# Attention inside the kernel: a small TensorE tile for each batch and head in place of block-diagonal operands

## The chip, the cores and the metric

One core of one Trainium2 chip runs the whole program. The metric is the device time of one execution in microseconds; several executions are made and the median is given. All data is f32.

## What is computed

A language-model tower of depth one: 4 x 512 tokens, 256 channels, 4 heads of 64. A row of a table is gathered for each token, then comes an attention-like layer with a recurrent state, and then a layer in which each token goes through one of 8 experts. The change lies in the attention layer. Cut to what matters:

```python
xx = shift(x) - x                      # xr, xw, xk, xv, xa, xg = x + xx * x_...
r, k, v = xr @ Wr, xk @ Wk, xv @ Wv
w = -softplus(-(w0 + tanh(xw @ w1) @ w2)) - 0.5
v = v + (v - v) * sigmoid(v0 + xv @ v1 @ v2)
a = sigmoid(a0 + xa @ a1 @ a2);  g = sigmoid(xg @ g1) @ g2
kk = normalised_per_head(k * k_k);  k = k * (1 + (a - 1) * k_a)
def step(S, ...):                      # S: 64 x 64 for each batch and head, over 512 steps
    sa = S @ (-kk)
    S = S * exp(-exp(w)) + outer(sa, kk * a) + outer(v, k)
    y = S @ r
y = (y - mean) / sqrt(var + 0.00064) * ln_w + ln_b      # per head
y = (y + sum(r * k * r_k) * v) * g @ Wo
```

## The kernel before, in words

The 512 steps are computed in chunks of 32 tokens (L). A chunk of all four batches is 128 rows; two chunks (CH) make a slab, and there are 8 slabs (SLABS). Within a chunk the recurrence is a triangular system of 32 x 32 for each batch and head; it is inverted by doubling, in four levels, and the state S is carried from chunk to chunk.

Each engine has its own program. All of them are written by the same function `pipeline`, which walks through one list of step names, `ORDER`, once for each turn. The letter ahead of a name says which slab the step works on in that turn (AHEAD): F, the layer norm and the transposes of the slab two ahead; P, all projections, gates, decay and the matrices of the slab one ahead; Q, the inversion and the state of this slab; O, norm and output of the slab behind. Engines wait for each other by semaphores only. So the order in which TensorE takes P and Q steps is the order of the list. Turns 1 to 4 are two rounds of a loop that holds two turns, the others are written out.

The steps that matter here, with their lines on TensorE: P.k, P.r, P.v (L877), the low-rank pairs (L883 down, L888 up), sums over heads (L894, with matrices of ones), P.tok (L997, six times four transposes that bring v, k and b to tokens), P.M (L977, products within a chunk for each batch and head), Q.X (L1009) and Q.T (L1018), the two matmul groups of one level of the inversion, Q.W (L1032, L1036), Q.A (L1048) and Q.S (L1059 to L1070), the right side, the solution, the new state and the output y, O.mean, O.var (L894), O.out (L1086). In a level, X is masked by VectorE (L680), T is added (L685) and transposed (L689), and ScalarE (L431) and GpSimd (L310) copy the blocks into `u_bd`. The operands of Q are block-diagonal: a unit holds four blocks of 32 x 32 on the diagonal of a 128 x 128 weight, two batches by two heads, and the slab has 8 units (UN). The same holds for the state, `state_bd`, with blocks of 64. In the last slab, where nothing else is left to do, `idle` puts matmuls without use (L903) between the steps of Q.

```python
                    for u in range(UN):
                        last = mm(ps[:, 4, u * L:(u + 1) * L], n_bd[par][:, u, :], t_c[:, u, :], start=True, stop=True)
```

## Time and profile before

| | us |
|---|---|
| three runs | 737.79, 733.80, 750.32 (median 737.79) |
| the profiled execution, first to last instruction | 741.3 |
| busy: TensorE matmul / weight load | 642.5 / 529.5 |
| busy: VectorE / ScalarE / GpSimd | 401.1 / 290.9 / 133.1 |
| mean granted clock of TensorE, share of 2.4 GHz | 0.886 |

A record is one instruction in the trace. An f32 matmul of the program appears as two MATMUL records with a LDWEIGHTS record each, a transpose as one. In a group, `128*128` is rows by columns of the stationary operand, `128x32` the streamed one.
### The profile page before, as it was taken

To read this page: it belongs to the slowest core of one execution; us is meant where nothing else is said; L and a number is where in the kernel's file an instruction comes from. 1 tells how busy PE (TensorE), PEld (TensorE's weight loads), DVE (VectorE), ACT (ScalarE), POOL (GpSimd) and SP (SyncE) were. 2 spreads that over 40 slices of the span, in tenths; PEclk is the share of its full clock that TensorE was granted. 3 is DMA by queue.
4 is the path that set the end of the run, shared out by engine and by line. 5 is a ranking of instruction groups with operands and counts; after the bars stand their busy time and mean duration, and the time that the engine had idled before them with its cause. 6 is when DMAs were issued, how large, how long until landed. Compare 5 with 4: busy or idle time off the path is not lost.

```text
span 741.3 us, 11776 instructions
## 1 busy us (share of the span) xinstructions
PE 642.5 (87%) x4339; PEld 529.5 (71%) x4340; DVE 401.1 (54%) x851; ACT 290.9 (39%) x556; POOL 133.1 (18%) x122
## 2 busy tenths in 40 slices
PE   0879899999998999999999999899948389999930
PEld 0658898888887889889888979899925145666620
DVE  6674576577676577677666765532163531222212
ACT  1554644354553464563545454511214003333300
POOL 6603102200400220130130040011000350000034
PEclk9979899599998989998979997999958558999985
DMA  7500000000000000000000000000009521212126
GB/s 216 187 1 1 1 2 1 0 2 1 1 1 3 1 1 1 1 1 2 1 1 1 1 1 1 2 1 1 1 2 399 203 92 44 63 64 64 56 60 188
DMA packets 20702, 30.95 MB, mean 42 GB/s; under 512 B 3832, under 2 KB 16432, under 8 KB 20528
## 3 DMA queue, kind: packets, MB, share of 16 engines
q1 hardware_dynamic: 18320, 23.99, 9.3%
q0 software_dynamic: 2336, 6.30, 2.8%
q8 instruction: 34, 0.56, 0.3%
q14 instruction: 12, 0.10, 0.0%
HBM read 20.06 MB, written 10.22 MB: 41 GB/s over the span
## 4 chain that ended last, share of the span: by engine, by line
PE 79%; DVE 8%; ACT 5%; issue 3%; POOL 2%; DMA 1%; SPq 1%; POOLq 0%; DVEq 0%
PE ps L1018 8%; PE ps L1009 7%; PE ps L877 6%; PE ps L1153 6%; PE ps L1170 5%; PE ps L888 5%; PE ps L883 5%; PE ps L1070 4%; PE ps L903 3%; PE ps L894 3%; PE ps L1048 3%; PE ps L997 3%; PE ps L1059 2%; PE ps L1133 2%; PE ps L1086 2%
## 5 line engine op out<-in xcount | busy, mean ns | idle before, releaser
L310 POOL TENSOR_TENSOR arena<-arena 64x512 f32<-64x512 f32 x40 | 48.9, 1224 | 401.0 <-DVE arena L689 201.4
L1018 PEld LDWEIGHTS ps<-arena 128*128 128x128 f32 x512 | 63.7, 200 | 11.4 <-DVE arena L680 5.6
L431 ACT COPY arena<-arena 32x256 f32<-32x256 f32 x80 | 32.3, 404 | 93.0 <-DVE arena L689 81.4
L1009 PEld LDWEIGHTS ps<-arena 128*128 128x128 f32 x512 | 64.5, 199 | 4.8 <-issue 2.6
L1018 PE MATMUL ps<-arena 128*128 128x32 f32 x512 | 65.4, 283 | 2.5 <-DVE arena L680 2.5
L1009 PE MATMUL ps<-arena 128*128 128x32 f32 x512 | 63.0, 278 | 0.0
L877 PE MATMUL ps<-arena 128*128 128x256 f32 x192 | 50.4, 410 | 6.5 <-issue 3.1
L877 PEld LDWEIGHTS ps<-arena 128*128 128x128 f32 x192 | 37.9, 204 | 13.0 <-issue 4.0
L448 ACT COPY arena<-arena 64x512 f32<-64x512 f32 x32 | 19.8, 618 | 68.2 <-PE ps L1070 68.0
L685 DVE TENSOR_TENSOR arena<-ps,arena 128x256 f32<-128x256 f32 x32 | 13.6, 424 | 59.1 <-PE ps L1018 59.0
L1153 PE MATMUL ps<-arena 128*128 x92 | 45.2, 614 | 0.1
L894 PE MATMUL ps<-arena 128*128 128x256 f32 x128 | 39.8, 439 | 5.6 <-ACT arena L452 3.3
L1170 PE MATMUL ps<-arena 128*128 x184 | 43.8, 379 | 0.8 <-ACT arena L496 0.8
L549 DVE SCALAR_TENSOR_TENSOR arena<-arena 128x256 f32<-128x256 f32 x96 | 41.0, 477 | 5.3 <-remote 2.7
L888 PE MATMUL ps<-arena 64*128 64x256 f32 (+2 forms) x128 | 41.7, 453 | 0.0
L839 DVE TENSOR_TENSOR arena<-ps,arena 128x512 f32<-128x512 f32 x23 | 15.9, 691 | 46.6 <-PE ps L1153 46.6
L1070 PE MATMUL ps<-arena 128*128 128x32 f32 x256 | 37.3, 269 | 0.0
L1170 PEld LDWEIGHTS ps<-arena 128*128 128x128 f32 x184 | 33.2, 190 | 5.3 <-issue 1.5
L883 PE MATMUL ps<-arena 128*64 128x256 f32 (+2 forms) x128 | 36.2, 408 | 0.0
L330 POOL DMA_INDIRECT arena<-sorted_o,arena x16 | 15.7, 979 | 112.8 <-DMA sorted_o<-arena 108.3
L680 DVE TENSOR_TENSOR arena<-ps,arena 128x256 f32<-128x256 f32 x32 | 13.4, 418 | 38.6 <-PE ps L1009 38.3
L894 PEld LDWEIGHTS ps<-arena 128*128 128x128 f32 x128 | 24.9, 211 | 12.8 <-issue 3.6
(189 smaller groups left out, 1305.9 us busy)
## 6 DMA issues: line engine op xcount, KB each, us to landing
arena<-W SPq DMA_DIRECT2D x16, 512.0 KB, 9.5
sorted_x<-arena SPq DMA_DIRECT2D x1, 2944.0 KB
arena<-sorted_x SPq DMA_DIRECT2D x23, 128.0 KB, 2.0
sorted_o<-arena SPq DMA_DIRECT2D x23, 128.0 KB, 1.7
arena<-b SPq DMA_DIRECT2D x1, 2048.0 KB, 20.3
out<-arena SPq DMA_DIRECT2D x16, 128.0 KB
arena<-W SPq DMA_DIRECT2D x4, 256.0 KB
arena<-consts SPq DMA_DIRECT2D x7, 64.0 KB
```

Of the source, the lines that this page charges most:

```text
L310: nc.gpsimd.tensor_tensor(u_bd[low, :, 64:128].rearrange("p u (q t) -> p u q t", q=2), (u_c if lvl else u_0[par])[low].unsqueeze(2).broadc ...
L431: last = nc.scalar.copy(u_bd[rows, :, L * q:L * q + L], (u_c if lvl else u_0[par])[rows])
L549: last = V.scalar_tensor_tensor(out=mix[j % 3][:, p, :], in0=xx[:, p].rearrange("p b t -> p (b t)"), scalar=vec[name][:, p:p + 1], in1=xT[ ...
L877: last = mm(ps[:, bank, m * NT:(m + 1) * NT], w[:, kt, m * 128:(m + 1) * 128], src[:, kt, :], start=kt == 0, stop=kt == 1)
L883: last = mm(ps[0:rows, bank, 0:NT], w[:, kt, :], src[:, kt, :], start=kt == 0, stop=kt == 1)
L888: last = mm(ps[:, bank, m * NT:(m + 1) * NT], w[0:rows, m * 128:(m + 1) * 128], src[0:rows, :], start=True, stop=True)
L894: last = mm(ps[:, bank, p * NT:(p + 1) * NT], w, src[:, p, :], start=True, stop=True)
L1009: last = mm(ps[:, 4, u * L:(u + 1) * L], n_bd[par][:, u, :], t_c[:, u, :], start=True, stop=True)
L1018: last = mm(ps[:, 5, u * L:(u + 1) * L], u_bd[:, u, :], x_c[:, u, :], start=True, stop=True)
L1070: last = mm(ps[:, 7, x + e * L:x + (e + 1) * L], state_bd[:, 2 * k + e, :], ar[par][:, k // 2, c * B + 2 * (k % 2) + e, L:2 * L], start=Fa ...
L1153: last = mm(ps[:, 2 + b, :], x_sT[b][:, p, :], W1_sb[:, bass.ds(e * (2 * HID) + p * HID, HID)], start=p == 0, stop=p == 1)
L1170: last = mm(ps[:, 6 + b, 0:C], hT[b][:, m, :], W2_sb[:, bass.ds(e * (HC * C) + m * C, C)], start=m == 0, stop=m == HC - 1)
```

## The change

Every batch and head gets a tile of TensorE of its own. The four batches of a chunk stand in partitions 0-31, 32-63, 64-95 and 96-127 (`quarter(b)`), and a product within a chunk is a matmul of 32 x 32 or 64 x 32 weights that reads and writes only those. Nothing is spread on a diagonal any more, and the copies that did so on ScalarE, GpSimd and VectorE are gone. r, k, kk, a and the decays lie by channel of one head (64) in two halves for the parity of the batch (`headed`), values, gates, y and z lie by token (`by_token`). The decay sums are matmuls against a triangle (P.cum) instead of a scan on VectorE. v is brought to mean zero per head (`vc`) ahead of the state, so y needs no mean; its variance is a square on ScalarE and a reduction on VectorE. In a level, T and its transpose U both come from matmuls, so VectorE doesn't transpose. low w and low a share one step (P.lwa). Part of S and y is computed ahead of the solution (in Q.A and Q.W). `idle` is gone. `set_up` puts one more wait, on a semaphore that is long past, ahead of a group of small tiles. The list ORDER is new.

The diff, cut to what the prediction speaks of:

```diff
-UN = 2 * CH * 2
+UN = CH * H
+GR = 2 * H
+SL = CH * L
...
-ORDER = """Q.start P.k O.mean P.r Q.X0 P.v Q.T0 P.lv P.vd O.var Q.X1 P.lw P.vg Q.T1 P.vgate O.z1 P.la P.w Q.X2 O.z2 P.lg P.a Q.T2
-P.vbd F.stats P.g O.out0 P.decay F.rstd Q.X3 P.norm F.xn O.out1 P.inv Q.T3 O.add Q.W0 F.xT Q.A0 P.tok0 P.tok1 P.key Q.S0 P.ar Q.W1
-P.rt P.kbd P.bonus Q.A1 P.tok2 P.tok3 P.bbd Q.S1 P.vcmp P.tok4 P.tok5 P.M F.xx P.ve Q.yT P.masks""".split()
+ORDER = """P.k Q.X0 O.sq Q.T0 P.r O.red Q.X1 P.v O.yn Q.T1 P.lv P.lwa Q.X2 P.kk P.vg O.zT Q.T2 P.wup P.lg Q.X3 F.stats P.a Q.T3
+P.g P.cum O.out P.decay F.rstd Q.W0 P.norm O.add Q.A0 F.xn P.key Q.S0 F.xT P.ar P.rt Q.W1 P.kP P.tokk Q.A1 P.bP P.tokb Q.S1 P.vc P.q F.xx
+P.M P.masks""".split()
...
-                    V.tensor_tensor(t_c, ps[:, 5, 0:UN * L].rearrange("p (u t) -> p u t", u=UN), t_c, ALU.add).then_inc(s["t_ok"], 1)
-                    dve.wait_ge(s["t_ok"], 5 * i + lvl + 2)
-                    dve.wait_ge(s["ubd_ok"], 5 * i + lvl + 1)
-                    dve.wait_ge(s["ubd2_ok"], 5 * i + lvl + 1)
-                    V.transpose(u_c.rearrange("p u t -> p (u t)"), t_c.rearrange("p u t -> p (u t)")).then_inc(s["u_ok"], 1)
...
+            def mul(out_, lhsT, rhs, start, stop):
+                return nc.tensor.matmul(out_, lhsT, rhs, start=start, stop=stop, skip_group_check=True)
...
+            def headed(w, src, bank):
+
+                for h in range(H):
                     for kt in range(2):
-                        last = mm(ps[:, bank, m * NT:(m + 1) * NT], w[:, kt, m * 128:(m + 1) * 128], src[:, kt, :],
-                                  start=kt == 0, stop=kt == 1)
+                        for e in range(2):
+                            to = ps[half(e), bank, :].rearrange("p (h b c t) -> p h b c t", b=2, h=H, c=CH)[:, h]
+                            last = mul(to, w[:, kt, half(h)], of_parity(src[:, kt, :], e), kt == 0, kt == 1)
                 return last
...
+            def to_tokens(src, bank):
+
+                for c in range(CH):
+                    for h in range(H):
+                        for b in range(B):
+                            g, e, u = h * 2 + b // 2, half(b % 2), c * H + h
+                            last = mul(ps[quarter(b), bank, u * HS:(u + 1) * HS], src[e, g, c, :], ident[e, e], True, True)
                 return last
-
-            def idle(i, count):
-
-
-                if isinstance(i, int) and i == SLABS - 1:
-                    pe.wait_ge(s["tok_ok"], 6 * SLABS)
-                    for _ in range(count):
-                        mm(ps[:, 0, 0:NT], cst["ones_bd"], w_sb["k"][:, 0, :], start=True, stop=True)
 
             def emit(step, i, par):
                 n = i + 1
...
-                    for src, bank in ((b_bd, 2), (k_bd, 3)):
-                        for p in range(2):
-                            for u in range(BLK):
-                                q, col = 64 * (u % 2), ((p * BLK + u) // 2) * 2 * L
-                                last = mm(ps[q:q + 64, bank, col:col + 2 * L], src[:, p, u, :], ar[par][:, p, u, :],
-                                          start=True, stop=True)
-                    last.then_inc(s["m_ps"], 1)
...
+                    for src, bank in ((bP, 2), (kP, 3)):
+                        for c in range(CH):
+                            for h in range(H):
+                                for b in range(B):
+                                    g, e, u = h * 2 + b // 2, half(b % 2), c * H + h
+                                    last = mul(ps[quarter(b), bank, u * 2 * L:(u + 1) * 2 * L], src[e, g, c, :], ar[par][e, g, c, :],
+                                              True, True)
+                        last.then_inc(s["m_ps"], 1)
...
                     for u in range(UN):
-                        last = mm(ps[:, 4, u * L:(u + 1) * L], n_bd[par][:, u, :], t_c[:, u, :], start=True, stop=True)
+                        for b in range(B):
+                            q = quarter(b)
+                            last = mul(ps[q, 4, u * L:(u + 1) * L], n_b[par][q, u, 0:L], u_m[q, u, :], True, True)
                     last.then_inc(s["x_ps"], 1)
-                    idle(i, 3)
...
                     for u in range(UN):
-                        last = mm(ps[:, 5, u * L:(u + 1) * L], u_bd[:, u, :], x_c[:, u, :], start=True, stop=True)
+                        for b in range(B):
+                            q = quarter(b)
+                            last = mul(ps[q, 6, u * L:(u + 1) * L], y_t[q, u, :], t_m[q, u, :], True, True)
+                            if lvl < 3:
+                                last = mul(ps[q, 6, (UN + u) * L:(UN + u + 1) * L], t_m[q, u, :], y_t[q, u, :], True, True)
                     last.then_inc(s["t_ps"], 1)
-                    idle(i, 5)
...
-                    for k in range(4):
-                        mm(ps[:, 4, k * HS:(k + 1) * HS], mak_bd[par][:, unit(k // 2, c, 2 * (k % 2)), :],
-                           v_cmp[par][:, unit(k // 2, c, 2 * (k % 2)), :], start=k == 0, stop=False, skip_group_check=True)
-                    for k in range(4):
-                        for e in range(2):
-                            last = mm(ps[64 * e:64 * e + 64, 4, k * HS:(k + 1) * HS], a_bd[par][:, k // 2, c * B + 2 * (k % 2) + e, :],
-                                      state[:, 2 * k + e, :], start=False, stop=k == 3, skip_group_check=True)
-                    last.then_inc(s["w_ps_c"], 1)
-                    idle(i, 3)
...
+                    for h in range(H):
+                        for b in range(B):
+                            q, u, at_h = quarter(b), c * H + h, half(h)
+                            mul(ps[q, 4, at_h], m_k[par][q, u, 0:L], vc[par][q, c, at_h], h == 0, False)
+                            mul(ps[q, 5, c * C + h * HS:c * C + (h + 1) * HS], m_k[par][q, u, L:2 * L], vc[par][q, c, at_h],
+                               c == 0 and h == 0, False)
+                    set_up()
+                    if c:
+                        pe.wait_ge(s["s_ok0"], n)
+                    for h in range(H):
+                        for b in range(B):
+                            g, e = h * 2 + b // 2, half(b % 2)
+                            last = mul(ps[quarter(b), 4, half(h)], ar[par][e, g, c, 0:L], state[e, b // 2, half(h)], False, True)
+                    last.then_inc(s["w_ps"], 1)
+                    for h in range(H):
+                        for b in range(B):
+                            g, e = h * 2 + b // 2, half(b % 2)
+                            mul(ps[quarter(b), 5, c * C + h * HS:c * C + (h + 1) * HS], ar[par][e, g, c, L:2 * L], state[e, b // 2, half(h)],
+                               False, False)
...
+                    for h in range(H):
+                        for b in range(B):
+                            q = quarter(b)
+                            last = mul(ps[q, 4, C + h * HS:C + (h + 1) * HS], t_m[q, c * H + h, :], w_s[q, half(h)], True, True)
                     last.then_inc(s["sa_ps"], 1)
-                    idle(i, 5)
...
+                        for b in range(B):
+                            q = quarter(b)
+                            mul(ps[half(b % 2), 6 + b // 2, half(h)], k_tok[par][q, c * H + h, :], vc[par][q, c, half(h)], h == 0, False)
...
-                    for k in range(4):
-                        u, x = unit(k // 2, c, 2 * (k % 2)), k * 128
-                        mm(ps[:, 6, x:x + 128], k_tok[par][:, u, :], v_e[par][:, u, :], start=True, stop=False)
-                        last = mm(ps[:, 6, x:x + 128], b_tok[par][:, u, :], sa_e[:, k, :], start=False, stop=True)
+                    set_up()
+                    pe.wait_ge(s[f"sa_ok{c}"], n)
+                    for h in range(H):
+                        for b in range(B):
+                            q = quarter(b)
+                            last = mul(ps[half(b % 2), 6 + b // 2, half(h)], b_tok[par][q, c * H + h, :], sa[q, half(h)], False, True)
...
+                    for h in range(H):
+                        for b in range(B):
+                            q = quarter(b)
+                            last = mul(ps[q, 5, c * C + h * HS:c * C + (h + 1) * HS], n_b[par][q, c * H + h, L:2 * L], sa[q, half(h)],
+                                      False, True)
```

The first place is the start of a turn on TensorE: P.k, then the first levels of the inversion. Before (a row is a line, an operation, output partitions by streamed columns, and a count in matmuls of the program):

```order
L877 MATMUL ps<-arena 128x256 x4
L1006 REGISTER_ALU
L1007 ISA
L1009 MATMUL ps<-arena 128x32 x8
L929 REGISTER_ALU
L877 MATMUL ps<-arena 128x256 x4
L1014 ISA
L1018 MATMUL ps<-arena 128x32 x8
```

And now, where all matmuls but transposes stand in the helper's line L801:

```order
L801 MATMUL ps<-arena 64x128 x16
L801 MATMUL ps<-arena 32x32 x96
L860 REGISTER_ALU
L801 MATMUL ps<-arena 64x128 x16
L801 MATMUL ps<-arena 32x32 x32
L865 REGISTER_ALU
L801 MATMUL ps<-arena 128x256 x4
L801 MATMUL ps<-arena 32x32 x64
```

X0 and T0 (8 matmuls each before) are 32 and 64, and stand together (the 96), where P.r or P.v stood between two steps of the inversion.

The second place is the end of a turn on TensorE, the second chunk's solution, its state and y, and the matrices P.M. Before:

```order
L1070 MATMUL ps<-arena 128x32 x2
L997 MATMUL ps<-arena 128x128 x8
L977 MATMUL ps<-arena 64x64 x32
L201 UNCONDITIONAL_BRANCH
L201 ISA
```

Now, from the sum with r_k (P.rt) on:

```order
L801 MATMUL ps<-arena 32x1 x32
L801 MATMUL ps<-arena 32x64 x112
L801 MATMUL ps<-arena 64x64 x16
L801 MATMUL ps<-arena 32x64 x32
L801 MATMUL ps<-arena 64x64 x16
L801 MATMUL ps<-arena 32x64 x80
```

The 112 are W1 (64), the token copies of k (32) and A1 (16); the last 80 are the y part of S1 (16) and P.M (64).

The third place is VectorE between the state of the second chunk and the end of the turn. Before, and then now:

```order
L701 TENSOR_TENSOR arena<-ps,arena 128x512
L705 TENSOR_TENSOR arena<-arena 128x512
L676 TENSOR_TENSOR arena<-arena 128x512
L591 TENSOR_TENSOR arena<-arena 128x16x31
L592 TENSOR_TENSOR arena<-arena 128x16
L549 SCALAR_TENSOR_TENSOR arena<-arena 128x256 x4
L658 TENSOR_TENSOR arena<-ps,arena 128x256
L662 TENSOR_TENSOR arena<-ps,arena 128x1024
```

```order
L635 TENSOR_TENSOR arena<-ps,arena 128x512
L639 TENSOR_TENSOR arena<-arena 128x512
L601 TENSOR_REDUCE arena<-arena 128x8
L603 SCALAR_TENSOR_TENSOR arena<-arena 128x512
L546 TENSOR_TENSOR arena<-arena 128x16x31
L547 TENSOR_TENSOR arena<-arena 128x16
L513 SCALAR_TENSOR_TENSOR arena<-arena 128x256 x4
L609 TENSOR_TENSOR arena<-ps,arena 128x512
L611 TENSOR_TENSOR arena<-arena 128x256
L614 TENSOR_TENSOR arena<-ps,arena 128x512
L616 TENSOR_TENSOR arena<-arena 128x256
L618 STREAM_TRANSPOSE arena<-arena 128x256
```

The reduction and the subtraction of v's mean (L601, L603) stand between the state and the mixes; the masks are narrower than before (no 1024 columns).

## Rows read from the trace of the kernel before

**Rows 1.** Stretches: start:end, length, busy (count) by engine, clock, DMA.

```profile
50.50:476.80 426.30, 415.48 (x3263) 365.13 (x3264) 279.28 (x527) 209.69 (x409) 71.33 (x56) 0.92 0.00 1
478.80:534.70 55.90, 55.90 (x403) 52.35 (x401) 17.67 (x33) 9.01 (x20) 5.79 (x5) 1.00 0.00 1
...
556.00:741.00 185.00, 135.02 (x547) 86.89 (x547) 57.06 (x177) 46.21 (x82) 31.27 (x32) 0.80 0.35 123
```

**Rows 2.** Line L977 in the source view: durations in ns, first and last start.

```profile
L977 PE MATMUL ps<-arena x512: 222/222/271, 50.5 to 476.8; 128*64 128x64 f32 x171
```

**Rows 3.** TensorE's waits from 50.5 to 476.8: total us, times, longest.

```profile
PE ps L1048 <- ACT arena L435: 4.1, 10, 0.7
PE ps L877 <- issue: 3.1, 1, 3.1
PE ps L1018 <- DVE arena L680: 2.5, 3, 1.9
PE ps L877 <- DVE arena L664: 0.4, 1, 0.4
```

**Rows 4.** Timeline of TensorE in the last slab: start, length, line, shapes, count.

```profile
482.86 1.87 PE L1009 MATMUL ps<-arena 128*128 128x32 f32 x16
484.57 1.54 PE L903 MATMUL ps<-arena 128*128 128x256 f32 x6
...
504.81 1.03 PE L1086 MATMUL ps<-arena 128*128 128x256 f32 x4
505.67 1.87 PE L1009 MATMUL ps<-arena 128*128 128x32 f32 x16
```

**Rows 5.** Timeline of TensorE around L977; the last row from its first 20 ns.

```profile
50.22 0.38 PE L997 MATMUL ps<-arena 128*128 128x128 f32 x2
50.53 2.08 PE L977 MATMUL ps<-arena 128*64 128x64 f32 x64
52.55 0.48 PE L877 MATMUL ps<-arena 128*128 128x256 f32 x1
...
50.53 0.28 PE L977 MATMUL ps<-arena 128*64 128x64 f32 x2
```

**Rows 6.** Stretches around a fall of the clock (columns as in rows 1).

```profile
125.10:128.50 3.40, 3.40 (x24) 2.70 (x22) 1.14 (x5) 1.25 (x4) 0.00 (x0) 1.00 0.02 5
128.50:145.60 17.10, 17.10 (x56) 13.41 (x55) 8.90 (x15) 5.78 (x13) 5.95 (x4) 0.50 0.00 0
```

**Rows 7.** Timeline of TensorE over the same stretches.

```profile
125.86 1.97 PE L1018 MATMUL ps<-arena 128*128 128x32 f32 x16
127.77 1.27 PE L883 MATMUL ps<-arena 128*64 128x256 f32 x4
...
138.38 3.62 PE L1018 MATMUL ps<-arena 128*128 128x32 f32 x16
141.81 2.05 PE L888 MATMUL ps<-arena 128*128 128x256 f32 x4
```

**Rows 8.** Groups by line: shapes, count, busy us, mean ns, idle before.

```profile
L1009 PE MATMUL ps<-arena 128*128 128x32 f32 x512 | 63.0, 278 | 0.0
...
L549 DVE SCALAR_TENSOR_TENSOR arena<-arena 128x256 f32<-128x256 f32 x96 | 41.0, 477 | 5.3 <-remote 2.7 <-issue 2.4
...
L680 DVE TENSOR_TENSOR arena<-ps,arena 128x256 f32<-128x256 f32 x32 | 13.4, 418 | 38.6 <-PE ps L1009 38.3
...
L701 DVE TENSOR_TENSOR arena<-ps,arena 128x512 f32<-128x512 f32 x16 | 11.1, 691 | 13.0 <-PE ps L1060 12.8
...
L467 ACT ACTIVATE arena<-arena 128x512 f32<-128x512 f32 x8 | 5.0, 630 | 0.3
```

**Rows 9.** Timeline of the end of the attention stage.

```profile
535.77 0.58 PE L1070 MATMUL ps<-arena 128*128 128x32 f32 x4
...
541.74 4.66 DVE L718 BATCH_NORM_STATS2 arena<-arena 128x6 f32<-128x256 f32 x14
...
553.09 0.69 DVE L734 TENSOR_TENSOR arena<-ps,arena 128x512 f32<-128x512 f32 x1 [3.87 <-PE ps L1086]
```

855 lines of the change are left out of this document (401 added, 454 removed).

## Prediction

> **What bounds the kernel now.** I read the stretches first [rows 1]. The attention stage in its steady state runs from 50.5 to 476.8 us, and TensorE is busy for 415.48 of those 426.30 us. So TensorE sets the pace there. Everything else stands below it: VectorE 279, ScalarE 210, GpSimd 71. The source view of L977 gives the period [rows 2]. Its 512 records are 8 bursts of 64, one per slab, and the first and the last burst start 426.3 us apart, so a turn takes 426.3 / 7 = 60.9 us. The waits confirm the first reading [rows 3]: in all seven turns TensorE waits 10.1 us for anything.
>
> What fills a turn is the number of TensorE records times their spacing. (An f32 matmul of the program leaves two records, a transpose one.) Starts in the timeline give the spacings [rows 4]. Sixteen records of L1009 (32 streamed columns over 128 stationary ones) start at 482.86 and the next line starts at 484.57: 0.107 us each. Four records of L1086 (256 streamed columns) take 0.86, so 0.215 each. The 64 records of L977 (64 stationary columns, two outputs side by side in partitions 0-63 and 64-127) run from 50.53 to 52.55: 0.0316 each [rows 5].
>
> Per turn that is 284 records at 0.11 (X and T 128, W, A and the state 64, the y part 64, transposes 28) = 31.2; 80 at 0.215 = 17.2; 96 at 0.0316 = 3.0. Together 51.4 of 60.9. The other 9.5: waits 10.1/7 = 1.4, about 20 changes of tile shape, and above all stretches at the lower clock. From 128.5 on TensorE works at half its clock for 17 us [rows 6], and 16 records of L1018 then take 3.43 (138.38 to 141.81) where they took 1.91 (125.86 to 127.77) [rows 7]. The mean clock of the seven turns is 0.92 [rows 1]; a sixth of the time at half clock loses about 34 us, 4.9 per turn.
>
> **The change, part by part.** No block-diagonal operands means small weights and many more matmuls. Records per turn afterwards:
>
> - Wide ones: v 8, low v 4, the joined low w and a 8 (two tiles side by side, so 4 in time), v, w and g gates 12, low g 4, out 8, the norm as one 512-column matmul 2 (4 in time): 44 x 0.215 = 9.5.
> - k, r and a: 80 records with 128 streamed columns on two 64-column tiles. One such stream alone is half of 0.215; side by side, as L977 does it, 0.055: 4.4.
> - Transposes of xn and z: 8 x 0.11 = 0.9.
> - Small ones: decay sums 64, r_k sum 64, token copies of k and b 128, M 128, X 256, T 448, W 256, A 128, S 128 = **1600**.
>
> Removed are the 128 wide X and T records, the 64 of the y part, 24 transposes, and three of four head sums. So 14.8 us stand fixed, and the price of the 1600 decides.
>
> **Price of a small record.** No row of before has it. From above: the mean of L977, 0.0316, which is two tiles wide. From below: L977 has two tiles, and each tile gets a record every 0.063. Two of its records start at once after a wait: a pair takes 0.28, one alone 0.27 [rows 2, 5]. So the starts of two tiles can lie 0.01 apart, and what spaces L977 is the tile and not the queue. Four tiles then give 0.0158 for the 832 records of 64 columns, and half, 0.0079, for the 768 of 32 columns or fewer: 19.2 us, a mean of 0.0120. I take 0.014, near the lower end, because the row shows the tile as its limit, with a little for the queue: 22.4 us. Both ends stay for the range: 19.2 and 50.6 us per turn.
>
> The Trainium skill, "TensorEngine Tiling (Array Packing)", section Instruction Overhead, speaks against this: each matmul has an overhead of about 60 cycles, and one streamed column lasts as long as 60. By that, taken as a gap between any two matmuls at 2.4 GHz (25 ns), the 1600 would cost 40 us per turn and the kernel would come to about 770 us; the trace has no 32-column stream on a small tile and cannot say.
>
> **Changes of shape.** Entering L977 costs 0.09 over the plain spacing: the last two transposes start at 50.22, at 0.11 each the next record would start at 50.44, and L977 starts at 50.53 [rows 5]. The changed order has about 36 such changes in a turn, 3.6 us.
>
> **Waits that the new order exposes.** VectorE operations of 512 columns take 0.69, of 256 columns 0.42 to 0.48, a ScalarE Exp of 512 columns 0.63, and the tail of a matmul, start to end, is 0.28 [rows 8]; I allow 0.1 per handing over. (1) T0 stands right behind X0 on TensorE, with nothing between: tail, one mask, handing over = 0.9. Queued behind it are P.r and all of the turn. (2) The sum r_k (rt) waits for norm, max, Ln, Exp, and four VectorE operations of 0.69: 0.27 + 0.69 + 1.26 + 2.76 + 0.7 = 5.7; beside it TensorE has 128 small records (1.8) and four transposes (0.4): 3.4 exposed. The second half of W and the token copies stand behind it. (3) The first X waits for the masks. From S1 on VectorE does the state (1.4), vc (1.3), xx (0.85), four mixes (1.9), masks with one transpose (2.65), in all 8.9 with handing over; TensorE has the rest of S, M and P.k, 0.45 + 1.8 + 1.8: 4.9 exposed. Sum 9.2. The other seven X and T steps are covered by P steps of 0.9 or more. If small records cost more, (2) and (3) shrink.
>
> VectorE itself: 28 operations at 0.69, 24 at 0.45 and small ones make 31 us a turn against 279.28/7 = 39.9, ScalarE falls from 30 to about 20, GpSimd stays near 10. None of them is a bound.
>
> A turn: 14.8 + 22.4 + 3.6 + 9.2 = 50.0; for the clock I keep 2 instead of 4.9, since there is less wide work to lose: **52.0**. Seven turns: 7 x 8.9 = 62 us less.
>
> **The ends.** The last slab's inversion has no other work beside it. Before, it fills with dummy matmuls (L903) and takes 478.8 to about 535.9, 57 us [rows 1, 9]. After: a level is X 0.9 + tail and mask 0.9, T 1.8 + 1.26, four levels 18; the two chunks 5.1 each; 29 us. Without dummies the clock will fall there; I take 24 less, not 28. Then the output: from y at 536.3 to 553.8 [rows 9], with two wide sums, ten passes and 14 statistics; after it has a square, a sum, three passes and the same statistics, 5 less. The first slab and everything behind 556 stay: the routing and expert code is the same, its 185 us too.
>
> Sum on the profiled execution: 741.3 - 62 - 24 - 5 = 650. Its span is 3.5 above the median of the three runs (737.79), so **647** on their scale.
>
> **The rivals.**
>
> *A, the queue sets the spacing.* If records cannot follow each other faster than at some spacing, whatever the tile, each nanosecond of it costs 1600 x 7 = 11.2 us. The gain is gone at 0.014 + 91/11.2 = 0.022; at 0.0316, the row's own value, the time is 844. Halfway, at 0.027, it is 647 + 13 x 11.2 = 793. For it: the highest rate anywhere in the trace is that of L977. Against: the close starts. Chance 0.27, of it slower 0.17, same 0.05, faster 0.05.
>
> *B, the clock.* From 125.1 to 128.5 TensorE was busy for all of 3.40 us and the clock fell after it [rows 6]. What ran was mostly short streams, L1018 with 32 columns [rows 7]. Small tiles stream over a quarter of the rows. If half of the time is at 0.5, the wide part gains 7.5 and the tile-bound small part about 8 per turn: 52 + 15.5 - 2 = 65.5, so 7 x 4.6 = 32 more, 29 less, on the scale of the median 741. For: the level falls without any idle time. Against: L1036 and L977 ran at full clock. The Trainium skill ("TensorE: Matmul & The Clock Gate", section HAM oscillation) blames idle gaps; rows 6 show a fall without one. Chance 0.12: slower 0.05, same 0.04, faster 0.03.
>
> *C, the chain through VectorE is longer than I count*. With every operation handed over at 0.25 instead of 0.1, some 45 of them, a turn grows by 7 us: 696. For: VectorE is strictly in order and the exposed waits all go through it. Against: its 31 us fill only 60% of a turn. Chance 0.10: faster 0.09, same 0.01.
>
> *D, my forecast*, 605 to 700, chance 0.51, all faster.
>
> **How the numbers follow.** A measurement of this kernel tells about 2% from no change, so faster is below 723 and slower above 752. Faster 0.51 + 0.09 + 0.05 + 0.03 = 0.68, same 0.10, slower 0.22. The lower end 605 is 0.0120 with half of the exposed waits (5 less each turn). The upper end reaches into A to 0.0254: 775, which leaves out about 0.14 above and 0.05 below.
>
> **What would show it.** In the changed profile the bursts of the T steps (128 records) should take 1.8 us, X 0.9, M 1.8. If T takes 3 or more at full clock, A holds. The period between two M bursts should be 52 with VectorE around 31 busy. Granted clock in the seven turns below 0.8 with T bursts near 1.8 would be B. VectorE waits for TensorE should be small at L622 and L630, and TensorE's waits should name the last of the key operations (L585) and the masks (L618). A busy ScalarE above 25 a turn, or a last slab over 40 us, would contradict my account of the ends. I am wrong altogether if tiles with the same output bank do not run side by side: then a small record costs more than L977's.

## The result, and the profile after

The changed kernel takes **705.9 us** (median of 4 runs, 700.7 to 710.3) against 737.9: a ratio of 0.957, 95% interval 0.950 to 0.963. That is faster by 4%, inside the whole range given (605 to 775, above the 700 up to which I counted it as my own case) and in its direction, but a third of the 91 us that I had forecast. Executions more than 1.5% above the fastest of their kernel are left out of the ratios, not of the medians. Two further sets of runs of it (after_again, control_3) gave ratios of 0.960 (0.948 to 0.971) and 0.938 (0.930 to 0.946), medians 705.1 and 698.3.

The profiled execution spans 708.5 us. From its page, first the busy times, then the queue that brings instructions, and two shares of the chain of work that ended last:

```profile
PE 524.5 (74%) x14419; PEld 404.3 (57%) x14420; DVE 296.9 (42%) x662; ACT 187.6 (26%) x372; POOL 133.2 (19%) x117
...
q8 instruction: 113, 1.85, 1.1%
...
PE 67%; issue 13%; DVE 12%; ACT 2%; POOL 2%; DMA 2%; SPq 2%; POOLq 0%; DVEq 0%
```

TensorE has 14,419 matmul records where it had 4,339, and is busy for less of the span. 13% of the chain is "issue", time in which an engine waited for nothing that the profile shows. The page of the kernel before has 3% there and 34 packets on q8.

The stretches, with the columns of [rows 1]. The first X burst of the first slab starts at 56.77 and that of the last slab at 464.58, so the first row is seven turns; then the last slab's inversion and chunks, then its output:

```profile
56.77:464.58 407.81, 325.53 (x12091) 264.83 (x12091) 191.13 (x367) 118.53 (x245) 73.88 (x55) 0.87 0.02 4
464.58:504.70 40.12, 26.84 (x1225) 22.80 (x1228) 8.48 (x15) 2.59 (x7) 0.00 (x0) 0.66 0.01 4
504.70:519.40 14.70, 5.12 (x28) 3.30 (x17) 8.90 (x21) 2.98 (x5) 0.00 (x0) 0.54 0.01 2
```

A turn is 407.8 / 7 = 58.3 us, where it was 60.9 and I had 52.0. TensorE is busy for 80% of it, where it was for 97%. Its waits over the seven turns, against [rows 3]:

```profile
PE ps L801 <- issue: 67.8, 71, 3.8
PE ps L801 <- DVE arena L618: 7.5, 7, 1.9
PE ps L801 <- ACT arena L432: 3.1, 5, 1.3
PE ps L801 <- DVE arena L513: 2.9, 5, 0.7
PE ps L801 <- DVE arena L622: 0.6, 1, 0.6
```

TensorE lost 82 us to waits instead of 10, and five sixths of it has no releaser. Where it sits is seen in the timeline of one turn's end (start, length, line, shapes, count, and in brackets the idle time ahead of the row):

```profile
275.04 1.38 PE L801 MATMUL ps<-arena 64*32 64x1 f32 x77
277.79 2.24 PE L801 MATMUL ps<-arena 32*32 32x64 f32 x127 [1.37 <-issue]
281.72 3.00 PE L801 MATMUL ps<-arena 64*32 64x64 f32 x127 [1.70 <-issue]
285.45 0.84 PE L801 MATMUL ps<-arena 64*32 64x64 f32 x13 [0.73 <-issue]
```

The idle times cut through bursts that wait for nothing: the last three rows begin in the middle of Q.W1, of P.tokk and of P.tokb. Between two of them stand 127 or 128 matmul records. Each record has its weight load, so that is 256 TensorE instructions. A packet on q8 is 16 KB, which would be 256 instructions of 64 bytes: the 113 packets x 256 are 28,900, about TensorE's own count of 28,839 (14,419 + 14,420), and the 34 of the kernel before are 8,704, against 8,679. In the trace such packets start at 275.61, 279.00 and 282.95, and TensorE goes on at 277.79, 281.72 and 285.45, some 2.5 us behind each. This gave the theory that the experiments were to test.

**Theory F**: TensorE runs dry. Its instructions come in blocks of 256 that cannot follow each other faster than every 3.5 us, and a block of small matmuls is worked off in 1.1 to 1.9. **Theory R**, the rival: the gaps belong to the array, its tiles or its clock, and the number of instructions does not matter.

### The profile page after: what moved, and what is told of

It reads as the page before. It is cut to its first block, busy times and chain, and to the rows that moved or that the text cites. A ratio compares the mean times of both kernels' runs of the same rounds, so it can differ in the third digit from the quotient of the medians.

```text
span 708.5 us, 31478 instructions
## 1 busy us (share of the span) xinstructions
PE 524.5 (74%) x14419; PEld 404.3 (57%) x14420; DVE 296.9 (42%) x662; ACT 187.6 (26%) x372; POOL 133.2 (19%) x117
## 3 DMA queue, kind: packets, MB, share of 16 engines
q8 instruction: 113, 1.85, 1.1%
## 4 chain that ended last, share of the span: by engine, by line
PE 67%; issue 13%; DVE 12%; ACT 2%; POOL 2%; DMA 2%; SPq 2%; POOLq 0%; DVEq 0%
PE ps L801 46%; PE ps L1119 6%; PE ps L1136 6%; PE ps L1099 2%; POOL arena L336 2%; PE ps L1127 1%; DVE arena L513 1%; PE ps L1073 1%; PE ps L1065 1%; SPq L229 1%; PE ps L1108 1%; PE ps L1048 1%; DVE arena L546 1%; PE ps L1080 1%; DMA arena<-g 1%
## 5 line engine op out<-in xcount | busy, mean ns | idle before, releaser
L801 PE MATMUL ps<-arena 32*32 32x32 f32 (+6 forms) x13808 | 376.9, 231 | 106.4 <-issue 83.2
L801 PEld LDWEIGHTS ps<-arena 32*32 32x32 f32 (+4 forms) x13808 | 307.0, 125 | 174.9 <-issue 147.0
L630 DVE TENSOR_TENSOR arena<-ps,arena 128x512 f32<-128x512 f32 (+1 forms) x32 | 19.9, 623 | 63.8 <-PE ps L801 63.6
L301 POOL TENSOR_TENSOR arena<-arena 128x512 f32<-128x512 f32 x8 | 9.5, 1186 | 179.5 <-ACT arena L364 179.5
L635 DVE TENSOR_TENSOR arena<-ps,arena 128x512 f32<-128x512 f32 x16 | 11.0, 687 | 71.4 <-PE ps L801 71.4
L1136 PEld LDWEIGHTS ps<-arena 128*128 128x128 f32 x184 | 33.2, 190 | 5.0 <-issue 1.5
L330 POOL DMA_INDIRECT sorted_x<-arena x16 | 15.6, 975 | 106.0 <-DVE arena L740 101.4
L766 DVE TENSOR_TENSOR arena<-ps,arena 128x512 f32<-128x512 f32 x23 | 15.9, 692 | 46.5 <-PE ps L1119 46.5
L622 DVE TENSOR_TENSOR arena<-ps,arena 128x256 f32<-128x256 f32 x32 | 13.6, 425 | 51.6 <-PE ps L801 51.6
L316 POOL TENSOR_TENSOR arena<-arena 128x512 f32<-128x512 f32 x8 | 17.5, 2192 | 84.8 <-ACT arena L420 84.8
L464 ACT COPY arena<-ps 128x256 f32<-128x256 f32 x23 | 8.6, 374 | 60.7 <-PE ps L1108 60.6
L1119 PEld LDWEIGHTS ps<-arena 128*128 128x128 f32 x92 | 16.1, 196 | 12.1 <-issue 12.1
L356 ACT COPY arena<-ps 128x512 f32<-128x512 f32 x8 | 4.7, 587 | 63.7 <-PE ps L801 53.7
L429 ACT COPY arena<-ps 128x256 f32<-128x256 f32 x16 | 6.0, 373 | 52.7 <-PE ps L801 52.7
L359 ACT COPY arena<-ps 128x512 f32<-128x512 f32 x8 | 4.7, 586 | 57.2 <-PE ps L801 57.2
L472 ACT COPY arena<-ps 128x512 f32<-128x512 f32 x23 | 13.5, 587 | 20.6 <-PE ps L1127 20.6
```

The source lines that it names most:

```text
L316: P.tensor_tensor(per_unit(rtv), per_unit(v2nd), rt.unsqueeze(2).broadcast_to([128, UN, HS]), ALU.mult).then_inc(s["rtv_ok"], 1)
L330: pool.indirect_dma_start(out=sorted_x[:, :], out_offset=bass.IndirectOffsetOnAxis(ap=place[:, t:t + 1], axis=0), in_=xn2[:, t, :], in_off ...
L472: nc.scalar.copy(hT[b], ps[:, 4 + b, :].rearrange("p (a t) -> p a t", a=HC)).then_inc(s["hT_ok"], 1)
L622: V.tensor_tensor(y_t, ps[:, 4, 0:UN * L].rearrange("p (u t) -> p u t", u=UN), cst["low"][:, L * lvl:L * lvl + L].unsqueeze(1).broadcast_t ...
L630: V.tensor_tensor(both, ps[:, 6, 0:wide * UN * L], both, ALU.add).then_inc(s[f"t_ok{lvl}"], 1)
L766: V.tensor_tensor(h_pre[b], ps[:, 2 + b, :], b1_sb[:, bass.ds(e * HID, HID)], ALU.add).then_inc(s["pre_ok"], 1)
```

## The experiments

For the comparisons I split each turn by the starts of the records: the spacing of each shape at full clock, what the half clock adds to it, changes of shape, gaps behind which stands a semaphore, and gaps over 0.3 us inside a burst without one. The turns here run from the second to the eighth norm matmul, six in all, us per turn. The wide records are the same in all of these kernels, so a difference of 1 us in that column is what the split gets wrong, and no finer reading rests on it:

| kernel | turn | wide | small | changes | clock | semaphore | gaps without | packets |
|---|---|---|---|---|---|---|---|---|
| changed (after_again) | 57.7 | 15.1 | 20.5 | 5.0 | 3.5 | 5.2 | 8.4 | 14.0 |
| half_count | 49.3 | 14.1 | 18.5 | 4.4 | 1.1 | 5.3 | 5.9 | 11.0 |
| double_columns | 57.6 | 14.1 | 23.8 | 4.4 | 1.7 | 6.3 | 7.2 | 14.0 |
| vector_transpose | 51.0 | 13.9 | 18.1 | 4.5 | 2.0 | 6.1 | 6.3 | 12.5 |
| gate_later | 58.9 | 14.9 | 20.3 | 4.9 | 4.2 | 7.2 | 7.4 | 14.0 |
| one_block_more | 61.2 | 14.1 | 21.6 | 5.0 | 4.7 | 6.0 | 9.8 | 15.0 |

### Fewer instructions, same columns; same instructions, more columns

```diff
 # half_count (X; T alike)
-for u in range(UN):
+for u in range(0, UN, 2):
-    mul(ps[q, 4, u * L:(u + 1) * L], n_b[par][q, u, 0:L], u_m[q, u, :], True, True)
+    mul(ps[q, 4, u * L:(u + 2) * L], n_b[par][q, u, 0:L], u_m[q, u:u + 2, :], True, True)
 # double_columns: u from 0 to 7 as before, each u writing the pair of places u - u % 2 and the next
```

> Edit: the changed kernel, but each X and T matmul streams 64 columns (two units) instead of 32, and there are half as many of them; the products are then not the reference's (each pair of units is multiplied by the first one's operand). Streamed columns are the same; 352 of about 1600 small TensorE records a turn are gone, with their weight loads 704 instructions, 2.75 blocks of 256. Theory F (TensorE runs dry because each 256 instructions need a fetched 16 KB block, and a block cannot come faster than every 3.5 us or so): the gaps of over 0.4 us on TensorE that no semaphore explains, 60.6 us in the seven turns of the changed kernel, fall below 30; instruction packets fall from 113 to about 93; time 655 to 672. Theory R (the gaps have to do with the array, its tiles or the clock, and the number of instructions does not matter): only the shorter bursts count, 704 records at 9.9 ns become 352 at 14.5 ns, 1.9 us less a turn, 13 in all, so about 693, with the gaps left at 50 to 60 us.

> Edit: the changed kernel, same number of X and T matmuls, but each streams 64 columns instead of 32 (it recomputes its neighbour's place as well, so the products are not the reference's). Instruction count unchanged, streamed columns of these 704 records a turn doubled: 9.9 ns to about 14.5 ns each, 3.2 us more array time a turn. Theory F: where a block's arrival sets the pace the longer work fits into the gap, so the gaps of TensorE without a semaphore fall from 60.6 to 40 to 50 us in the seven turns and the time grows by only 5 to 15 us: 711 to 721. Theory R: the whole of it is added, 3.2 x 8 = 26, 732, with the gaps as before.

Measured: half_count 626.9 us, ratio 0.851 (0.841 to 0.861). double_columns 694.9, ratio 0.942 (0.933 to 0.952). The page's line on the instruction queue, and the six turns, of half_count and then of double_columns:

```profile
q8 instruction: 91, 1.49, 1.0%
...
74.20:370.00 295.80, 244.24 (x8301) 196.43 (x8293) 165.66 (x324) 103.72 (x216) 62.35 (x47) 0.97 0.02 4
```

```profile
q8 instruction: 113, 1.85, 1.1%
...
84.40:429.80 345.40, 283.64 (x10407) 232.13 (x10405) 166.78 (x324) 103.52 (x215) 64.01 (x47) 0.95 0.02 4
```

Taking 352 records a turn away and leaving their columns takes 8.4 us from a turn, of which the small records are 2.0, the gaps 2.5 and the clock 2.4. The packets fell by 22, as 704 instructions less in each of eight slabs say. Doubling the columns of 704 records a turn adds 3.3 us of array time and nothing to the turn. R said 693 and 732 for the two, and both are far off. F's numbers missed too. It gave 655 to 672 and 711 to 721, so half_count gained more than it allows and double_columns did not lose the 5 to 15 us that it allows; and half_count's gaps, which it put below 30 us in seven turns, are 5.9 a turn, 41. What I had left out is in the table: in both the clock stands higher, 0.97 and 0.95 against 0.89, worth 2.4 and 1.8 us a turn. double_columns lies 3 to 11 us below the changed kernel in the other sets of runs, with no control of its own, so I read no gain from it, only that the added work cost nothing.

### A whole block more

First I tried it with 256 satisfied semaphore waits a turn, in both kernels (a satisfied wait is one on a semaphore that has long reached its value).

```diff
 def emit(step, i, par):          # TensorE; eight wide steps
+    if step in ['P.v', 'P.lv', 'P.lwa', 'P.wup', 'P.lg', 'P.g', 'O.out', 'P.norm']:
+        for _ in range(32):
+            pe.wait_ge(s["zeroed"], 1)
```

> Edit: the changed kernel with 32 further waits on a semaphore that is long satisfied ahead of each of 8 wide steps of TensorE (values, low ranks, gates, output, norm), 256 instructions a turn with no array work: one block more a turn. The result stays the reference's. Theory F: one instruction packet more a turn, 113 to about 121, and a turn grows by 1 to 3.6 us, 8 to 28 in all: 714 to 734. Theory R: a turn grows by the waits' own issue time alone, which the same waits in the kernel before give (their cost there is the control).

> Edit: the kernel before with the same 256 satisfied waits a turn, 32 ahead of each of 8 wide steps of TensorE. The result stays the reference's. It has about 1000 instructions a turn, 4 blocks in 60.9 us, so by theory F the fifth block is hidden and only the waits' own issue time shows: 256 at 0.01 us or less, under 3 us a turn: 738 to 755. Theory R says the same of this kernel; the difference to the changed kernel with the waits is what tells them apart: F gives the changed kernel the larger increase, R gives both the same.

Measured: waits_after 794.7 us, ratio 1.074 (1.063 to 1.086); waits_before 740.5, ratio 1.005 (1.001 to 1.008). The direction is F's, but 89 us are three times what it allows, so the experiment did not price a block. The traces show two reasons. The 32 waits ahead of a step became 16 instructions: TensorE's sequencer, the part that issues its instructions, has 1,024 more records than without them (1,787 against 763, and 1,784 against 760), and q8 has four packets more (117 and 38), not the eight that I had counted on. So only half a block a turn was added. And such an instruction is itself not cheap: in a row they start 0.106 us apart in both kernels, which is 128 x 0.106 = 13.6 us a turn. A turn of waits_after is 14.6 us longer (72.3 against 57.7), so the changed kernel pays for nearly all of it; the kernel before pays 0.3 a turn. So it was done again with work that costs the sequencer no more than what is there:

```diff
 # one_block_more, P.rt
-for c in range(CH):
+for c in (0, 1, 0, 1, 0, 1):
```

> Edit: the changed kernel, but the sum r_k (P.rt) is done three times over into the same place, which leaves the result as it is: 128 more records a turn with one streamed column, at 8.4 ns each 1.08 us of TensorE, and 256 more instructions, exactly one block, in the part of the turn where small bursts follow each other. Theory F: a block costs its arrival and not its work, 3.5 to 4 us a turn, 28 to 32 in all, 733 to 738. Theory R: 1.1 a turn, 8.6 in all, 714.

> Edit: none, the changed kernel, as the control of the two others on this chip: 700 to 710.

Measured: one_block_more 731.6, ratio 0.980 (0.973 to 0.988); control_3 698.3, ratio 0.938 (0.930 to 0.946). The ratios differ by 0.042 of the kernel before's 743 us: **31 us for eight blocks, 3.9 a block** (2.9 to 4.9 by the two intervals; the medians differ by 33), with 1.1 of array time in each. F had 28 to 32, R 8.6. The q8 line has 121 packets, eight more, and a turn is 61.2 us, 3.5 longer than in after_again and 4.1 longer than in control_3 (57.1).

### The rate by itself

```diff
 # rates, ahead of TensorE's first step: the same 512 matmuls (1024 records), 32 columns on 32x32
+for k in range(512): matmul(*one(k))                             # L805
+with pe.Fori(0, 16): for k in range(32): matmul(*one(k))         # L808, half a block
+with pe.Fori(0, 8): for k in range(64): matmul(*one(k))          # L811, one block
+with pe.Fori(0, 2): for k in range(256): matmul(*one(k))         # L814, four blocks
```

> Edit: the changed kernel with a measuring section ahead of TensorE's work: 512 f32 matmuls of 32x32 by 32 columns over the four row tiles in a straight line (1024 records, 2048 instructions, 8 blocks), the same 512 as a loop of 16 turns of 32 (half a block), of 8 turns of 64 (one block) and of 2 turns of 256 (4 blocks), then 128 matmuls of 128x128 by 128 columns. The result stays the reference's. Theory F: the straight line runs at 3.5 us a block, 27 ns a record, in steps of 128 records with a gap behind each, and the wide ones run without gaps; whether the short loops run from what is already there (9 to 10 ns a record but for the jump) or fetch each turn is open and is what this looks for. Theory R: the straight line runs at 9.9 ns a record without gaps.

The timeline of TensorE in that section:

```profile
42.35 1.93 PE L805 MATMUL ps<-arena 32*32 32x32 f32 x128 [2.08 <-issue]
45.81 1.93 PE L805 MATMUL ps<-arena 32*32 32x32 f32 x128 [1.53 <-issue]
49.27 1.93 PE L805 MATMUL ps<-arena 32*32 32x32 f32 x128 [1.53 <-issue]
52.73 0.69 PE L805 MATMUL ps<-arena 32*32 32x32 f32 x34 [1.53 <-issue]
53.19 14.80 PE L808 MATMUL ps<-arena 32*32 32x32 f32 x1024
68.08 11.18 PE L811 MATMUL ps<-arena 32*32 32x32 f32 x1024
79.33 1.49 PE L814 MATMUL ps<-arena 32*32 32x32 f32 x155
82.80 1.27 PE L814 MATMUL ps<-arena 32*32 32x32 f32 x128 [1.98 <-issue]
86.27 1.93 PE L814 MATMUL ps<-arena 32*32 32x32 f32 x128 [2.19 <-issue]
90.28 7.49 PE L814 MATMUL ps<-arena 32*32 32x32 f32 x613 [2.09 <-issue]
```

This settles it. In a straight line every 128 records stand 3.46 us apart (45.81, 49.27, 52.73), or 4.0. That line ran at half clock, where the records alone take 1.7 us (13.4 ns each); the loop of four blocks begins at full clock, where they take 1.1, and the step is again 3.47 (82.80, 86.27). The same matmuls as a loop of one block take 11.18 us for all 1024, at full clock, with a single packet at the loop's start (69.16) and 0.3 us for each jump back. The four-block loop has gaps on its first turn; its second, 512 records, is within the last row and runs through from 91.85 to 97.58 at 11 ns each, in part at half clock. So the gaps are the arrival of new instructions, and what was fetched can be run again without them.

> Edit: the changed kernel with another measuring section ahead of TensorE's work, behind the loading of the weights: in straight lines 512 records each with 32, 64 and 128 streamed columns on 32x32 tiles; then loops of 3 turns whose bodies are 6, 7.5 and 9 blocks of 256 instructions. The result stays the reference's. Theory F: with 32 and 64 columns (9 and 15 ns a record, 1.2 and 1.9 us a block) both straight lines take the same 3.5 us a block; with 128 columns (28 ns or more, 3.6 us a block) the gaps go. The 4-block loop of the run before had no gaps on its second turn; a body too large for what TensorE keeps has gaps on every turn, the others on the first alone. The main loop of the kernel before has about 8 blocks and fetches on every turn, so I expect the limit between 6 and 9 blocks. Theory R: the spacing follows the streamed columns from the start, 9, 15 and 28 ns, without gaps.

The straight lines of 64 and of 128 columns in rates_2 (here both L808), then the loop of six blocks from the last block of its first turn on. The row of 384 ends with 86 records of that loop's start, and the row of 1774 with records of the next loop's:

```profile
41.23 1.99 PE L808 MATMUL ps<-arena 32*32 32x64 f32 x128 [0.74 <-issue]
44.97 1.99 PE L808 MATMUL ps<-arena 32*32 32x64 f32 x128 [1.75 <-issue]
48.71 0.70 PE L808 MATMUL ps<-arena 32*32 32x64 f32 x35 [1.75 <-issue]
...
57.20 9.54 PE L808 MATMUL ps<-arena 32*32 32x128 f32 x384 [0.32 <-issue]
...
87.78 16.99 PE L808 MATMUL ps<-arena 32*32 32x32 f32 x1774
106.78 0.41 PE L808 MATMUL ps<-arena 32*32 32x32 f32 x27 [2.00 <-issue]
```

With 64 columns a block still takes 3.74 us (41.23, 44.97, 48.71), with 128 columns the records alone take 3.5 us a block (27 ns each) and the gap behind a block shrinks to 0.3. The second and third turns of the six-block loop (768 records each, to 102.5) run without a gap but for the jump. The loops of 7.5 and of 9 blocks had an idle time of 1.5 us or more behind every 128 records on all three turns. So of a loop TensorE keeps at least 6 blocks and fewer than 7.5. The attention loop of the changed kernel has 27 or 28 blocks (two turns) and that of the kernel before about 8, so both fetch everything each time; the kernel before needs a block only every 15 us and never notices.

### The order

```diff
-... P.a Q.T3 P.g P.cum O.out ... P.tokk Q.A1 ...
+... P.a Q.T3 P.cum O.out ... P.tokk P.g Q.A1 ...
```

P.g then waits for tokk_ok, the next P.lv for g_ok and F.xT for lg_ok.

> Edit: the changed kernel, same instructions, in another order: P.g (4 wide records, 0.75 us, few instructions for their time) stands behind P.tokk, between bursts of small records, instead of ahead of P.cum among wide ones. The result stays the reference's. Theory F: the 0.75 us and the change of shape come to lie in the gaps of the tail, 3 to 8 us less in all: 698 to 703 if the control gives 706. Theory R: no change within 2 us.

Measured: 715.1, ratio 0.968 (0.948 to 0.989), control 0.960 (0.948 to 0.971): the intervals overlap, so neither the gain of 3 to 8 us nor a loss is shown. In the profile the gaps did fall, by 1.0 us a turn, as F says. But waits on semaphores rose by 2.0. Of gate_later over its six turns:

```profile
PE ps L801 <- DVE arena L513: 7.4, 5, 2.3
...
PE ps L801 <- ACT arena L423: 4.7, 6, 0.8
```

The first, for the mixes of VectorE, was 2.8 in after_again. The second is new. L423 is ScalarE's copy of the key tokens, and P.g stands right behind the burst that feeds it. I had counted neither. As a test of F it is inconclusive.

### The last slab

```diff
 # before_no_fill: the dummies of L903 left out
 # after_fill, ahead of each Q.X and Q.T of the last slab
+    idle(i, 2)     # ones_bd x w_sb["k"], 256 columns, into bank 0
```

> Edit: the kernel before without the dummy matmuls (L903) of the last slab; the result stays the reference's. It prices the last slab's part of the change. If the dummies only keep the clock up, the last slab's X, T, W and A work (about 170 wide records, 20 us) then runs at half clock where it is not waiting, and the last slab (478.8 to 535.9) becomes 0 to 8 us longer. If they are in the way of the chain, it becomes up to 10 us shorter. In all 728 to 748.

> Edit: the changed kernel with two dummy matmuls (128x128 by 256 columns, 0.43 us each at full clock, 0.86 at half) ahead of each X and each T of the last slab, 16 in all; the result stays the reference's. In the changed kernel the last slab's inversion, 464.6 to 488.2 of its profile, runs wholly at half clock. By my prediction's term (4 us lost there for the clock) this gives 2 to 4 us back if the dummies fit into the waits of 0.8 to 1 us: 701 to 704. If theory F carries the last slab too (gaps of blocks 13 us of its 53), the clock does not matter and nothing changes: 704 to 708; if the dummies are in the way of the chain, 3 to 6 us more.

Measured: 750.0 us (733.1 to 755.4) and 693.6 (681.2 to 700.0); no ratio for either. So I read them by their stretches. First before_no_fill from its last L977 burst to its last product, then after_fill and control_3 from X0 to their last product:

```profile
470.80:536.20 65.40, 57.74 (x311) 54.83 (x307) 19.30 (x35) 10.51 (x23) 5.79 (x5) 0.58 0.00 1
```

```profile
449.65:486.93 37.28, 27.75 (x1255) 22.47 (x1256) 8.48 (x15) 2.59 (x7) 0.00 (x0) 1.00 0.02 4
```

```profile
453.70:495.10 41.40, 26.77 (x1228) 22.65 (x1228) 8.52 (x15) 2.59 (x7) 0.00 (x0) 0.67 0.01 4
```

The kernel before took 59 us for the first of these stretches (476.8 to 535.9), so its dummies were worth 6 there, inside the 0 to 8 expected, though the median of 750.0 lies outside the 728 to 748 that went with it. In the changed kernel they lift the clock from 0.67 to 1.00 and save 2.8 us against the 40.1 above and 4.1 against control_3, as the clock term had it (2 to 4). With the clock full, some 1250 records still need their ten blocks. Each of these lengths is one profile; the rest of the distance between 693.6 us and the 701 to 704 expected lies ahead of the last slab.

### A version that is faster than both

The second product of T0 to T2 only makes the transpose of the first. VectorE can do that with one more operation.

```diff
 # vector_transpose, TensorE
-if lvl < 3:
-    last = mul(ps[q, 6, (UN + u) * L:(UN + u + 1) * L], t_m[q, u, :], y_t[q, u, :], True, True)
 # VectorE
-V.tensor_tensor(both, ps[:, 6, 0:wide * UN * L], both, ALU.add)
+V.tensor_tensor(t_flat, ps[:, 6, 0:UN * L], t_flat, ALU.add)
+V.transpose(tu[par][:, 1].rearrange("p u t -> p (u t)"), t_flat)     # lvl < 3, behind a wait
```

> Edit: the changed kernel computes the same, but the second product of T0 to T2 (the transposed operand) is not made on TensorE; VectorE adds the first product (256 columns) and transposes the sum in 32x32 blocks. 192 records and 384 instructions a turn go, 1.5 blocks; VectorE has 0.45 + 0.45 where it had 0.69 between a T and the next X, covered by P steps. Theory F: array time 192 x 9.9 ns = 1.9 us less a turn, gaps 2 to 3 us less, clock about 1 less: 5 a turn, about 665 (655 to 678). Theory R: 1.9 less a turn, 0.6 more where the longer VectorE pair shows, 690 to 697.

> Edit: none, the changed kernel as it is, on the same chip as the next kernels. Both theories: 700 to 712, with 113 instruction packets and about 60 us of TensorE gaps without a semaphore in the seven turns.

Measured: **653.3 us, ratio 0.889 (0.874 to 0.904)**, against 0.960 (0.948 to 0.971) for the changed kernel beside it. Its six turns:

```profile
81.80:387.60 305.80, 247.22 (x9257) 200.44 (x9253) 166.82 (x342) 103.47 (x215) 66.80 (x47) 0.94 0.02 4
```

That is below F's 655 to 678 and far below R's 690 to 697. A turn went from 57.7 to 51.0: 2.4 off small records, 2.1 off gaps, 1.5 off the clock, and 0.9 more on semaphores (the rest is in the columns that the split separates badly). 1.5 blocks at the 3.9 us of one_block_more are 5.9 of these 6.7, and q8 has 101 packets, 12 less.

> Edit: the changed kernel with the transposes of T0 to T2 on VectorE (vector_transpose, 653) and two dummy matmuls ahead of each X and T of the last slab (after_fill); the result stays the reference's. The last slab of after_fill is 2.9 us shorter from X0 to the last product than that of the changed kernel, by its profile; the other 9 us between its time and the control's lie ahead of it, mostly in the start (5.6), which the edit does not touch. So I expect 653 - 3 = 650 (643 to 656), and not the 12 less that the two medians differ by (641).

Measured: **647.2 us, ratio 0.871 (0.865 to 0.878)**, with the fill in the last slab as well. Of all kernels that leave nothing of the computation out it has the lowest time, 13% under the kernel before. How much of that is the fill is seen only in the last slab, which takes 33.6 us from X0 to the last product where vector_transpose takes 37.7. The sets of runs do not separate the two: 647.2 is 51 us under its own control (698.3), and 653.3 is 52 under its own (705.1). That it is also the number that I forecast for the changed kernel is chance.

## Why the prediction missed the size

**The failed step is a term that the sum of a turn did not have.** "What fills a turn is the number of TensorE records times their spacing" was true of the kernel before, where a block of 256 instructions was worked off in some 15 us. For the changed one I priced a record by its array tile alone. Its instructions have a price too, 3.5 us or more for each 256, and in a burst the larger of the two counts. That is 9.0 us a turn which my sum did not have, 63 in seven turns. Point by point, per turn, from X0 to X0:

| term | forecast | measured |
|---|---|---|
| wide records | 14.8 | 14.4 |
| 1600 small records | 22.4 | 20.5 |
| changes of shape | 3.6 | 4.9 |
| waits on semaphores | 9.2 | 5.4 |
| half clock | 2.0 | 4.1 |
| gaps without a semaphore | none | **9.0** |
| sum | 52.0 | 58.3 |

**The price of a small record was right** and rival A is refuted as I had stated it. 32x32 tiles with 32 columns take 8.9 to 9.9 ns a record, those with 64 columns 14.1 to 16; that is the low end (19.2 us a turn) that I had derived from one tile being the limit of L977. At full clock X bursts take 0.56 us, T bursts 1.27 and M 1.85, gaps aside (I had 0.9, 1.8 and 1.8; the burst of 128 in T would have been 3 or more by A). The rule of the Trainium skill ("TensorEngine Tiling (Array Packing)", Instruction Overhead), taken as 25 ns between any two matmuls, does not hold across tiles: 8.9 ns here. Yet A's remark that a queue could set the pace came nearer to the truth than my forecast did: gaps included, a small record costs (20.5 + 9.0) / 1600 = 18 ns on the average, where the gain would have been gone at 22. What sets it is a rate over 256 instructions, not a spacing between two. The Trainium skill ("Trainium Architecture — The Big Picture", The software stack) has instructions of 64 bytes, which agrees with 16 KB for 256; of how the streams reach the engines that section has only the load ahead of the run, and the trace here shows 113 packets during the run.

**The waits.** T0 behind X0 waits 0.7 (forecast 0.9). rt waits 0.9 (3.4) and X0 for the masks 1.5 (4.9), since what stands ahead of them on TensorE got longer by the gaps. The copies between W, A and S cost 1.6, which I had at nothing. VectorE has 27 us of a turn (31 forecast), ScalarE 17 (20). Rival C is refuted: with longer hand-overs the waits would have grown by 7 us a turn, and they are 5.4 where 9.2 were forecast. The rows of waits above name VectorE for 11 us only in all seven turns; T0's wait behind X0 and part of the others stand there under "issue", as the waits for copies do, so "issue" alone does not tell a missing instruction from a short wait.

**The clock** (rival B) is real but small: 4.1 us a turn instead of 2, at a mean of 0.87 where I had warned of below 0.8. What lowers the clock is not shown. The gaps alone do not: one_block_more, with the longest gaps, has 4.7, and half_count, with the shortest, 1.1, but double_columns and after_again stand idle for the same time, 13.5 and 13.6 us a turn, and lose 1.7 and 3.5 to the clock. A mean of 0.87 is a quarter of the time at the lower level, where B supposed half.

**The ends.** From X0 to the last product the last slab takes 40.1 us (41.3 in the profiles of after_again and control_3) where I had 29, and 33 with the clock. That is over the 40 us that I had named as a sign against my account. The kernel before takes 53.2 from its X0 (482.86) on: my 57 began at 478.8, with 4 us ahead of X0 that the 29 did not have, so 4 of the 24 us forecast were never there. The measured gain is 13. The timeline names the same cause as in the turns:

```profile
464.58 1.08 PE L801 MATMUL ps<-arena 32*32 32x32 f32 x64 [1.87 <-DVE arena L618]
466.24 1.78 PE L801 MATMUL ps<-arena 32*32 32x32 f32 x114 [0.58 <-issue]
469.79 0.46 PE L801 MATMUL ps<-arena 32*32 32x32 f32 x14 [1.77 <-issue]
471.15 1.08 PE L801 MATMUL ps<-arena 32*32 32x32 f32 x64 [0.91 <-DVE arena L630]
```

The gap between 114 and 14 records of one T0 burst is a block's edge, and the slab has about 10 us of such gaps. Its output takes 14.7 instead of 17.7 (3 less, 5 forecast). The first X0 starts at 56.77 us in both kernels, so nothing is gained or lost ahead of it, as forecast.

Together, on the spans, from X0 to X0 in both: turns 18.3 us less (62 forecast), last slab 13.1 (24), output 3.0 (5) and the rest 1.6 more (0): 33 less, where 91 were forecast.

One sum of the prediction does not come out, without bearing on the result: its lower end of 605 is said to be 0.0120 with half of the exposed waits, which is 647 - 22 - 35 = 590.

## What to carry to other kernels

Count the instructions of an engine as well as its work. Where new code runs on TensorE (a straight line, or a loop too long to be kept), 256 instructions (128 f32 records with their weight loads) cost whichever is longer, their array time or about 3.5 to 4 us, and that is 27 ns a record or more: cutting one operation over the array into many small tiles pays only as far as it stays above that, so take the version with the fewest matmuls, even if another engine must do an operation more. An "issue" gap in the middle of a burst, every 128 records, together with a packet on the instruction queue, is the sign; a loop of up to 6 blocks (96 KB) does not pay this after its first turn.

## What the runs showed of the hardware

- Records on four separate 32x32 tiles follow each other at 8.9 ns at full clock (32 columns, f32; the X bursts of the changed kernel), 13.4 at half; with one column on 64x32 tiles at 8.4.
- A loop of up to 6 blocks runs its later turns without gaps (one packet, at 89.28, in its last 1536 records), one of 7.5 blocks fetches on each turn (rates_2).
- In the straight lines of rates and rates_2, blocks of instructions arrive at steps of 3.46, 3.74 or 4.0 us, at either clock. Why these three values is open.
- A wait instruction of TensorE that is long satisfied takes 0.106 us of its sequencer. In the kernel before 128 of them a turn cost 0.3 us a turn, in the changed one 11 by the medians and 14.6 by the profile. My reading, which no run tests by itself, is that they are hidden only while issued matmuls are still waiting for the array.
- The start varies by 6 us between profiles of the changed kernel and its variants (first norm matmul at 34.8 to 40.8) without any edit there. It was not pursued.
